# A two-layer graph kernel on one core: indirect gathers issued in fours, each four held until the four before it has landed

## What is computed

```
edge_input = concatenate([x[src], edge_attr])                  # layer 0
messages = gelu(edge_input @ mW1 + mb1) @ mW2 + mb2
gates = sigmoid(gelu(edge_input @ gW1 + gb1) @ gW2 + gb2)
aggregated = segment_sum(messages * gates, dst)
h = x + gelu(concatenate([x, aggregated]) @ uW1 + ub1) @ uW2 + ub2
x1 = layernorm(x + layernorm(h) * ln_g + ln_b)
out = segment_sum((x1 @ W)[row] * norm, col) + b               # layer 1, row/col = src/dst and loops
x2 = layernorm(x1 + out)
```

## Time and profile before

| | |
|---|---|
| median of the timed runs | 1552.31 us (1551.43 to 1552.61) |
| span of the profiled execution | 2435.8 us |
| pass 1, to the last of its gathers, in the profile | 2.8 to 1414.7 us |
| pass 2, from its first gather, in the profile | 1564.1 to 2435.8 us |
| busy in the span | PE 68%, POOL 47%, DVE 46%, ACT 23% |

### The profile page before, as it was taken

The page is one execution under the profiler, slowest core; times in us unless marked ns, Lnnn a source line. Parts: engine busy times, 40 slices in busy tenths (PEclk is TensorE's granted clock), DMA queues, the critical chain, the costliest instruction groups (busy, mean ns, idle before and its releaser), DMA issues.

```text
span 2435.8 us, 29257 instructions
## 1 busy us (share of the span) xinstructions
PE 1667.9 (68%) x10142; PEld 1463.5 (60%) x10143; DVE 1117.0 (46%) x2955; ACT 555.5 (23%) x989; POOL 1150.0 (47%) x1225
## 2 busy tenths in 40 slices
PE   2067777777777777777777794766546878656867
PEld 1056666666666666666666683665545767655757
DVE  4145555555555555555555573713223224131343
ACT  1023333333333333333333342200000001000010
POOL 7635555555455555444455514225444433454441
PEclk8578888888898898888899896877767878787988
DMA  3133333343333333333333432423223534343431
GB/s 77 36 86 92 91 109 100 97 111 95 94 107 95 99 96 107 91 99 110 100 94 95 111 107 75 154 79 113 80 85 101 171 121 155 103 130 110 158 121 55
DMA packets 161685, 250.39 MB, mean 103 GB/s; under 512 B 54899, under 2 KB 128627, under 8 KB 152316
## 3 DMA queue, kind: packets, MB, share of 16 engines
q1 hardware_dynamic: 111372, 173.90, 20.9%
q0 software_dynamic: 38784, 59.65, 11.9%
q10 hardware_dynamic: 11376, 14.90, 2.1%
HBM read 160.45 MB, written 87.88 MB: 102 GB/s over the span
## 4 chain that ended last, share of the span: by engine, by line
PE 53%; another core or an unknown queue 23%; issue 16%; ACT 4%; DVE 2%; ACTq 1%; POOL 0%; DVEq 0%; DMA 0%; POOLq 0%
PE ps_hid L659 10%; PE ps_hid L770 7%; PE ps_xt L770 6%; PE ps_xt L693 5%; PE ps_win L863 4%; PE ps_xt L631 4%; PE ps_bt L764 3%; PE ps_hid L656 3%; ACT shared L999 3%; PE ps_hid L693 2%; PE ps_win L604 2%; PE ps_hid L742 1%; PE ps_xt L742 1%; ACTq L348 1%
## 5 line engine op out<-in xcount | busy, mean ns | idle before, releaser
L534 POOL DMA_INDIRECT rows<-in_x_nat,idx x782 | 742.4, 949 | 669.9 <-PE ps_xt L631 388.8
L534 POOL DMA_INDIRECT rows<-x1s_table,idx x398 | 375.4, 943 | 525.2 <-DVE acc L1552 346.4
L659 PE MATMUL ps_hid<-mats,large 128*128 128x192 f32 x1568 | 390.4, 380 | 0.0
L656 PE MATMUL ps_hid<-b_split,ones_b 128*128 128x384 bf16 x392 | 150.5, 384 | 291.6 <-ACT shared L999 208.0
L659 PEld LDWEIGHTS ps_hid<-mats,large 128*128 128x128 f32 x1568 | 333.0, 231 | 26.0 <-issue 9.1
L959 ACT ACTIVATE large<-ps_hid 128x768 f32<-128x768 f32 x196 | 158.8, 810 | 445.4 <-remote 229.7
L693 PE MATMUL ps_xt<-shared 128*128 128x275 f32 x768 | 219.3, 409 | 49.8 <-DVE shared L1337 43.7
L656 PEld LDWEIGHTS ps_hid<-b_split,ones_b 128*128 128x128 bf16 x392 | 42.4, 108 | 323.4 <-ACT shared L999 227.5
L1299 DVE TENSOR_SCALAR ps_fix<-squash 128x8 f32<-128x8 f32 x98 | 16.6, 169 | 454.2 <-issue 255.7
L1337 DVE TENSOR_TENSOR shared<-cell,ps_fix 128x1650 f32<-128x1650 f32 (+3 forms) x136 | 221.3, 1627 | 0.0
L604 PE MATMUL ps_win<-hot,large 128*98 128x80 f32 x1568 | 166.0, 258 | 54.6 <-DVE acc L1251 36.6
(11 more groups left out here) (192 smaller groups left out, 2125.8 us busy)
## 6 DMA issues: line engine op xcount, KB each, us to landing
b_table<-shared SPq DMA_DIRECT2D x288, 275.0 KB
large<-b_table SPq DMA_DIRECT2D x72, 1100.0 KB
rows<-in_x_nat,idx POOLq DMA_INDIRECT x782
large<-in_edge_t ACTq DMA_DIRECT2D x96, 128.0 KB
rows<-x1s_table,idx POOLq DMA_INDIRECT x398
large<-in_x_t SPq DMA_DIRECT2D x7, 336.0 KB
x_nat<-in_x_nat SPq DMA_DIRECT2D x7, 336.0 KB
x1s_table<-x_nat ACTq DMA_DIRECT2D x45, 48.0 KB
```

The lines of the kernel that those rows point to most:

```text
L534: nc.gpsimd.indirect_dma_start(out=rows[slot][:, k, :], out_offset=None, in_=table, in_offset=bass.IndirectOffsetOnAxis(ap=idx[:, TG * g + ...
L656: nc.tensor.matmul(ps_hid[j][:, 0:2 * HC], ones_b[:, :], flat(b1_split[:, :, :]), start=True, stop=False)
L659: mm = nc.tensor.matmul(ps_hid[j][:, HC * q:HC * (q + 1)], feat[u][:, P * m:P * (m + 1)], w1[:, :], start=False, stop=(q == 1))
```

## The change

In `gathers` a hook is called ahead of the fifth gather of a group. In pass 1 and pass 2 the hook waits until the first four gathers of this group have landed. Ahead of a group's first gather there is a further wait, until all gathers of the group before have landed (from group 2 of pass 1, and from the second group that pass 2 gathers after the early ones). So no more than four gathers are under way at a time. Order, sizes and slots stay.

```
@@ gathers
-            def gathers(g, slot, table, rows_sem, n):
+            def gathers(g, slot, table, rows_sem, n, half_ready=None):
                 last = g == NG - 1
                 for k in range(TG - (REST if last else 0)):
+                    if k == TG // 2 and half_ready is not None:
+                        half_ready()
                     nc.gpsimd.indirect_dma_start(
@@ pass 1
                     pool.wait_ge(s_xt, g - SLOTS + 1)
-                gathers(g, g % SLOTS, t["x_nat"], s_rows, g % SLOTS)
+                if g > 1:
+                    pool.wait_ge(s_rows[(g - 1) % SLOTS], group_rows((g - 1) // SLOTS, (g - 1) % SLOTS))
+                gathers(g, g % SLOTS, t["x_nat"], s_rows, g % SLOTS,
+                        lambda: pool.wait_ge(s_rows[g % SLOTS], 16 * (TG * (g // SLOTS) + TG // 2)))
@@ pass 2
                         pool.wait_ge(s_acc2, PLACE[GATHERED[i - SLOTS]] + 1)
+                    if i > NE:
+                        pool.wait_ge(s_rows2[(i - 1) % SLOTS], group_rows((i - 1) // SLOTS, (i - 1) % SLOTS))
                     if i >= NE:
-                        gathers(g, slot_of(i), x1s_table, s_rows2, i % SLOTS)
+                        gathers(g, slot_of(i), x1s_table, s_rows2, i % SLOTS,
+                                lambda: pool.wait_ge(s_rows2[i % SLOTS], 16 * (TG * (i // SLOTS) + TG // 2)))
```

## The result

The changed kernel takes 2271.53 us (median, 2267.75 to 2275.52), the kernel before 1551.87 us: a ratio of 1.4628 with a 95% interval of 1.4611 to 1.4646. It is 720 us slower, 2.46 us for each of the 292 waits. The direction and the mechanism were forecast (1946 us, range 1790 to 2050); the price of a wait, 1.35 us, was little over half of what it is.

What follows compares the result with a forecast made beforehand. POOL was taken to bound the timed run nearly end to end, with nothing hiding its waits. 1552 us plus 292 waits at 1.35 us, 394 us, gave 1946 us, range 1790 to 2050.

Steps and rivals of the forecast that it cites:

- the price of a wait: Both passes: each added wait costs POOL 1.35 us, from landing and wake-up less the 0.30 us gap, plus traffic.
- POOL is the bound: Timed run, nearly end to end: POOL sets the time; its 735 us of waiting exist in the profile alone.
- the sum of 1553.1 us: POOL alone, never waiting: 2.8 us start, 1212 gathers at 1.248 us, some 2 us small instructions, 35.6 us end.
- 1305 us of full-clock work: PE in both passes: busy time times granted clock, 966 x 0.86 + 593 x 0.80, so hardly the only bound.
- the stalls of 950 us: Unknown-queue and issue time on the profile's chain, 39% of the span, taken as lost to the recording.
- hidden anyway: Rival, both passes: PE's 14.95 us groups and DVE's 346.4 us cover the waits; time 1552 us, chance 0.02.
- The count of 292: Added waits: 97 mid-group and 96 ahead of groups in pass 1, 50 and 49 in pass 2.
- Nothing hides it: Timed run, both passes: no other engine or slot covers the waits, so all 394 us add to the time.
- PE takes over: Rival, pass 1: idle pieces lower PE's clock; under 0.67 PE decides, 2086 us at 0.6; chance 0.03.
- The upper bound of 1.77 us: Highest cost of one wait, from a 48 KB store's landing 2.5 us after issue; would give 2069 us.
- The reading that I set aside: Rival, both passes: gathers land 2.1 us behind their descriptors, 2.08 us a wait, 2159 us; chance 0.04.
- What would show it: Signs in the changed profile: 1.3 to 2 us gaps ahead of first and fifth gathers, span growing under 100 us.

Runs made afterwards that it cites:

- iotas of 171 us: Kernel before, with eight small iotas on POOL ahead of each four gathers from group 3 on and no added waits: 1719.97 us against 1551.94.
- the order swapped: Changed kernel with the two waits ahead of a group in the other order, landing first, then slot, in both passes: 2128.59 us.
- the twos: Changed kernel with each two gathers held until the two before have landed, 584 waits: 2696.59 us, ratio 1.7335 to the kernel before.
- the quiet one: Changed kernel with b_table stores and loads cut to 25 columns, except each buffer's first load: 2097.26 us, 1.87 us a wait.

## Why the prediction was right in its mechanism and wrong in its size

*POOL is the bound.* Right: iotas of 171 us cost 168, and a wait in either pass costs its idle time. That the sum of 1553.1 us met the median within 1 us was partly luck. Its end piece, 35.6 us from the slower execution, is 18.0 us at full speed (1533.33 to 1551.3), and POOL's waits for DVE and for the last store, 15.0 us, which it put at nothing, make up for it. PE was a closer second than the prediction's 1305 us of full-clock work: the sum left out the 108 us that PE works between the passes, and at full speed PE is busy for 92% of the time. The argument that led from the profile to it was half wrong: I put the stalls of 950 us down to the recording, and they were, by the second profile of the kernel before, real time of a slower execution. The rival "hidden anyway", which took the profile's waits at their word, would have been near the truth there: at that speed the changed kernel is even faster than the one before.

*The count of 292.* Right: with the order swapped the profile shows 193 and 99 waits.

*Nothing hides it.* Right: in every row of the table the timed growth is POOL's idle time, within 35 us, and never less by more than 9 us. PE, busy for 92% before, did not become the bound in any run, so that "PE takes over" falls: the mean granted clock did sink, from 0.98 to 0.85 in the changed kernel and 0.79 in the twos, but not to the 0.67 from which the rival decided, and PE is busy for 72% and 63% there.

*The price of a wait.* Here the prediction failed. I took 1.35 us, of which 1.14 (1.17 + 0.27 - 0.30) from the isolated early gather and 0.21 as an allowance for traffic. Measured are 2.46 us. The terms, per wait: 1.14 from the rows; +0.39, because the semaphore lands 1.56 us after the descriptors and not at 1.17, the middle of the 1.05 to 1.30 us that I read from the DMA engines' last activity in the earlier trace rows; +0.24 (136 x 0.505 / 292) for the second wait instruction at a group's head, a term that I did not have at all; +0.60 for the traffic, where I allowed 0.21. Together 2.37 us, 692 us of the 720. Most of what is left is that 1.56 us is a median and the mean even without traffic is 1.59 to 1.67 us. The sentence that failed is "I take 1.35 us: the isolated gather's, and a tenth of a microsecond or two for the traffic". The upper bound of 1.77 us was no bound: a median of a store does not bound the mean of the last of four gathers, whose tail reaches 6.7 us in the waits of the changed kernel.

*The page weighed against it.* The Trainium skill (DMA: Bandwidth & Descriptors, section "Anatomy of one DMA — SWDGE (gpsimd) path") gives 2.0 us plus the bytes over 436 GB/s, an estimate of 2.1 us for such a gather. From issue to landing the changed kernel's profile has 2.6 us (median) and the quiet one's 2.5, 0.94 of it for the descriptors, which the page calls small. The reading that I set aside, 2.1 us behind the descriptors, would have given 2159 us. That is nearer to the 2271 measured, but by luck: the trace has 1.56 us there, and the reading holds neither the second wait instruction nor the traffic.

*What would show it.* The gaps were to be 1.3 to 2 us: those within a group are 1.74 and 1.78, those at a head are not. The loss over 520 us names the price of a wait as the failed step, which is so. The span was to grow by under 100 us; it shrank from 2435.8 to 2266.0 us, since the first profile was of the slower speed.

## What to carry to other kernels

Before pricing a wait on a stream of transfers, sum the issuing engine's work alone against the timed run: where the two agree, each stop costs its full latency, and slots or depth don't help. Such an agreement can be chance in its terms, as 18 us of it were here, so test it with added work of known length, as the iotas did. Take that latency from the semaphore's landing and not from the last byte, add the release, and put the condition that is met last first in program order when an instruction has two. Waits moved back by four gathers or more, which let at most twelve be under way, cost 4 us in all, where the strict ones cost 720.

When a profile's span and the timed runs differ by hundreds of microseconds, profile again before explaining the difference.

## What the runs showed of the hardware

- An indirect gather of 128 rows of 384 bytes: 0.944 us of descriptor writing on GpSimd, 1.248 us from start to start, its semaphore 1.56 us (median, quiet) after the descriptors, 0.34 us behind the last packet. Beside the stores and loads the mean is 1.77 to 2.86 us, and the median in three of the four places still 1.56 to 1.61.
- An instruction with two waits: 0.764 us from the event to its start if the separate instruction ahead holds the condition that is met last, 0.259 us if the gather itself does. Swapping the two lines was worth 143 us of 2271, of which 69 us are this.
- The same program at two speeds, 1552 and 2390 to 2435 us, the latter with results of TensorE that come microseconds after the end of the matmuls in the record (4.7 us in the earlier trace rows) and a mean granted clock of 0.83 to 0.84 instead of 0.98. One chip had both, at different times. The changed kernel took 2271 and 2275 us beside the two. What sets the speed stays open.
